# Attention values as f16 products for half of the units, and a new order of the step's four queues

## Chip, core, metric

The kernel runs on one core of a Trainium2 chip. The metric is the device time of one execution in microseconds (us), lower is better. The engines are PE (matmul, with its weight loads shown apart as PEld), DVE (vector), ACT (scalar activation), POOL (GpSimd) and SP, which issues most of the DMAs. Each engine runs its own instructions in the order written, and waits on semaphores for the others.

## What is computed

The input is x of 8 batches, 512 rows and 256 columns. After a layer norm, an attention with a compressive memory runs over four segments of 128 rows, with 16 heads of 64. An FFN of three coupled cycles follows. The change touches the attention alone:

```
scores  = mask(q @ k.T * scale)
att_dot = softmax(scores) @ v
att_mem = (elu(q) + 1) @ M / ((elu(q) + 1) @ Z)
M, Z    = M + (elu(k) + 1).T @ v,  Z + sum(elu(k) + 1)
out     = (gate * att_mem + (1 - gate) * att_dot) @ Wo
x       = x + layernorm(out)
```

## The kernel before

**Tiles.** Two batches make a pair, so there are 4 pairs of 4 segments, which gives 16 steps m = 4 * bp + s. A step handles 32 units (2 batches by 16 heads), in four groups g of 8 units. A group has two halves of 4 units, and its units are also split by par, 0 or 1, the two units that share one pair of 64 partitions. v has 65 columns a unit: 64 of v and a column of ones, so that the sum of the softmax comes out with the product.

**What a group does.** PE transposes q and k of the group (`turn`), ACT and DVE split them into f16 high and low parts, and `scores` makes the masked scores from 24 f16 products into the two PSUM banks `s_bank`, par 0 and par 1. DVE takes the row maxima, ACT the exponentials (`probs`), PE transposes them back into `s_bank` (`turn_probs`), and ACT copies them to `PT` (`take_p`). `read_out(g, half)` then multiplies PT with v for 4 units in f32 (L1305), the queries with the memory M (L1311), and after the second half the keys with v for the new memory (L1319). DVE divides (`divide`), POOL mixes with the gate (`gated`) and makes elu(k) + 1 (`elu_k`).

**What else is in a step.** The projections of the next step's q, k and v (`project` 0 to 5, 12 f16 products of 512 columns each, taken by DVE's `take_x`, L915), the transposes of the finished attention of the step before (`to_rows` on DVE, A0 to A3 on PE), the output projection Y (32 records at L1347), its layer norm and residual (y, x2), the next rows' layer norm (N) and the transposed result (F). They share two banks `t_bank` in turn, in the order of `STEP_JOBS`. The last step (m = 15) has no projections.

**What sets the order.** Every queue is written out by hand in the functions `step` of PE, DVE, ACT and POOL. There is one `s_bank`, so `scores` of a group waits until the probabilities of the group before have been copied. There is one `x_bank`, so each projection waits for the transpose of the one before. A step is counted below from its first score product (L1270 for g = 0). Step 9 lies at 509.43 to 562.61 us.

Of the kernel before, what the change touches and what calls it, by code (L numbers as in the profile page):

```python
# [45 lines left out]
STEP_JOBS = ["Q1", "K1", "A0", "A1", "A2", "A3", "Y", "Q2", "K2", "N", "Q3", "K3", "F", "Q0", "K0"]  # L46
# [18 lines left out]
def infini_block_kernel(nc, x, Wq, Wk, Wv, Wo, betas, memory0, z0, cw1, cb1, cw2, cb2, cw3, cb3,  # L65
                        cw4, cb4, gw1, gb1, gw2, gb2, gw3, gb3, adaptive_range, out):
    ctx = ExitStack()
    with ctx:
# [51 lines left out]
        PT = alloc(GU * P).rearrange("p (h j i) -> p h j i", h=2, j=GP)  # L120
# [4 lines left out]
        attT = alloc(2 * H * DK).rearrange("p (w j r) -> p w j r", w=2, j=8)  # L125
# [104 lines left out]
        p_done = sem("p_done")  # L230
# [77 lines left out]
        o_done, od_done = sem("o_done"), sem("od_done")  # L308

# [14 lines left out]
        with nc.Block() as block:  # L324
# [77 lines left out]
            def _(pool):  # L402
# [71 lines left out]

                def y_dev(bp, s):

                    deviation(r_rs, r_mv, y_stat, y_rstd, bp * NSEG + (s + 1))
# [10 lines left out]
                def step(bp, s):  # L488
                    m = bp * NSEG + s
                    elu_k(bp, s, 0)  # L490
                    if m > 0:
                        gated(*before(bp, s), 3, 0)
                        gated(*before(bp, s), 3, 1)
                    elu_k(bp, s, 1)
                    gated(bp, s, 0, 0)
                    gated(bp, s, 0, 1)
                    if m < NT - 2:
                        deviation(n_rs, n_mv, n_stat, n_rstd, m + 3)
                    y_dev(bp, s)
                    gated(bp, s, 1, 0)  # L500
                    residual(bp, s)
                    elu_k(bp, s, 2)
                    x2_dev(bp, s)
                    gated(bp, s, 1, 1)
                    elu_k(bp, s, 3)
                    gated(bp, s, 2, 0)
                    gated(bp, s, 2, 1)
# [73 lines left out]
            def _(act):  # L581
# [41 lines left out]
                def take_q(bp, s, g):  # L623
# [8 lines left out]
                    act.activation(eq, eq, ACT.Exp, scale=-1.0).then_inc(qk_act, 1)  # L632
                    b, n = t_job(bp, s, f"K{g}")
# [21 lines left out]
                def probs(bp, s, g):  # L655
                    G = 4 * s + g
                    for par in range(2):
                        act.wait_ge(m_done, bp * 32 + (2 * G + par + 1))
                        for j in range(GP):
                            last = act.activation(Pr[:, par, j, :], s_bank[:, par, j * P:(j + 1) * P], ACT.Exp,  # L660
                                                  bias=negm[:, par, j:j + 1])
                        last.then_inc(e_done, 1)

                def take_p(bp, s, g):
                    for par in range(2):
                        act.wait_ge(pt_full, bp * 32 + 8 * s + 2 * g + par + 1)
                        last = act.activation(PT[:, par, :, :].rearrange("p j i -> p (j i)"), s_bank[:, par, :],  # L667
                                              ACT.Copy)
                    last.then_inc(p_done, 1)
# [24 lines left out]
                def step(bp, s):  # L694
                    ahead, last = bp * NSEG + s < NT - 2, bp * NSEG + s == NT - 1
                    exp_k(bp, s, 0)
                    probs(bp, s, 0)
                    take_p(bp, s, 0)
                    if s == 0 and bp > 0:
                        reset(*before(bp, s), 3)  # L700
                    take_q(bp, s, 1)
# [3 lines left out]
                    probs(bp, s, 1)  # L705
                    take_a(t_job(bp, s, "A2"), 2)
                    take_a(t_job(bp, s, "A3"), 3)
                    take_p(bp, s, 1)
                    reset(bp, s, 0)
                    take_y(t_job(bp, s, "Y"))  # L710
                    take_q(bp, s, 2)
                    exp_k(bp, s, 2)
# [4 lines left out]
                    probs(bp, s, 2)  # L717
                    take_p(bp, s, 2)
                    take_q(bp, s, 3)
                    exp_k(bp, s, 3)  # L720
                    reset(bp, s, 1)
                    take_f(t_job(bp, s, "F"), bp * NSEG + (s - 1))
                    probs(bp, s, 3)
# [878 lines left out]
```

## Time and profile before

| what | value |
|---|---|
| median of three runs | 1071.33 us (1067.8 to 1072.13) |
| the profiled execution's own time | 1069.13 us |
| span from first to last instruction | 1067.3 us |
| first score product, m = 0 | at 34.97 us |
| first score product, m = 15 | at 826.97 us |
| mean granted TensorE clock | 0.98 of full speed |

The rest of the span is the start (weights and the first projections) and the FFN at the end. A busy time in the profile is the union of an engine's instructions. An f32 product appears as two records, so four products of `read_out` are "x8". Matmuls overlap in the records, so what a group costs is read from its start to the next group's start.

### The profile page before, as it was taken

To read this page: it belongs to the slowest core of one execution; us is meant where nothing else is said; L and a number is where in the kernel's file an instruction comes from. 1 tells how busy PE (TensorE), PEld (TensorE's weight loads), DVE (VectorE), ACT (ScalarE), POOL (GpSimd) and SP (SyncE) were. 2 spreads that over 40 slices of the span, in tenths; PEclk is the share of its full clock that TensorE was granted. 3 is DMA by queue.
4 is the path that set the end of the run, shared out by engine and by line. 5 is a ranking of instruction groups with operands and counts; after the bars stand their busy time and mean duration, and the time that the engine had idled before them with its cause. 6 is when DMAs were issued, how large, how long until landed. Compare 5 with 4: busy or idle time off the path is not lost.

```text
span 1067.3 us, 20188 instructions
## 1 busy us (share of the span) xinstructions
PE 989.8 (93%) x7748; PEld 697.6 (65%) x7748; DVE 780.9 (73%) x1400; ACT 634.6 (59%) x1364; POOL 577.8 (54%) x688
## 2 busy tenths in 40 slices
PE   5999999999999999999999999999999889999971
PEld 2677777776777777767777777777777765343431
DVE  6868686867787877777777777686868463588685
ACT  4756565556566564556565646574746354687872
POOL 4456565446565654456565634565656352455573
PEclk9999999999999999999999999999999899999995
DMA  7100000000000000000000000000000100300025
GB/s 187 32 21 1 21 2 20 3 22 1 21 2 21 2 20 2 21 2 21 1 21 2 21 2 20 2 21 1 12 2 10 24 11 10 157 1 1 1 44 115
DMA packets 17038, 23.92 MB, mean 22 GB/s; under 512 B 7472, under 2 KB 9264, under 8 KB 16432
## 3 DMA queue, kind: packets, MB, share of 16 engines
q1 hardware_dynamic: 15472, 18.58, 6.3%
q10 hardware_dynamic: 1472, 4.06, 1.1%
q8 instruction: 62, 1.02, 0.4%
q14 instruction: 32, 0.26, 0.1%
HBM read 13.97 MB, written 8.65 MB: 21 GB/s over the span
## 4 chain that ended last, share of the span: by engine, by line
PE 72%; DVE 18%; POOL 3%; ACT 3%; issue 3%; POOLq 0%; DVEq 0%; ACTq 0%
PE ps L1241 18%; PE ps L1347 11%; PE ps L1305 6%; PE ps L1282 5%; PE ps L1488 4%; PE ps L1475 4%; DVE arena L915 4%; PE ps L1311 3%; PE ps L1292 3%; PE ps L1332 3%; PE ps L1470 3%; PE ps L1257 3%; DVE arena L875 2%; PE ps L1319 2%; DVE arena L940 2%
## 5 line engine op out<-in xcount | busy, mean ns | idle before, releaser
L1241 PE MATMUL ps<-arena 128*128 128x512 f16 x1152 | 266.7, 382 | 5.1 <-DVE arena L892 3.0
L660 ACT ACTIVATE arena<-ps,arena 128x128 f32<-128x128 f32 x512 | 139.4, 387 | 96.1 <-DVE arena L940 96.1
L1241 PEld LDWEIGHTS ps<-arena 128*128 128x128 f16 x1152 | 110.3, 98 | 126.1 <-DVE arena L915 4.5
L915 DVE STREAM_TRANSPOSE arena<-ps 128x1024 f32<-128x1024 f32 x96 | 145.6, 1517 | 24.6 <-PE ps L1241 22.5
L468 POOL TENSOR_TENSOR arena<-arena 128x256 f32<-128x256 f32 x128 | 93.2, 729 | 123.2 <-DVE arena L950 82.0
L1305 PE MATMUL ps<-arena 128*128 128x65 f32 x1024 | 135.9, 276 | 5.9 <-ACT arena L667 4.8
L1305 PEld LDWEIGHTS ps<-arena 128*128 128x128 f32 x1024 | 127.4, 192 | 18.8 <-ACT arena L667 8.3
L867 DVE BATCH_NORM_STATS2 arena<-arena 128x6 f32<-128x256 f32 x100 | 36.9, 410 | 121.0 <-ACT arena L686 120.2
L1347 PE MATMUL ps<-arena 128*128 128x256 f32 x544 | 121.9, 382 | 0.0
L453 POOL TENSOR_TENSOR arena<-arena 128x512 f32<-128x512 f32 x48 | 73.2, 1525 | 86.6 <-ACT arena L653 86.6
L1347 PEld LDWEIGHTS ps<-arena 128*128 128x128 f32 x544 | 102.0, 190 | 15.7 <-ACT arena L674 0.8
L472 POOL TENSOR_TENSOR arena<-arena 128x256 f32<-128x256 f32 x128 | 95.3, 745 | 10.0
L421 POOL TENSOR_TENSOR arena<-arena 128x2 f32<-128x2 f32 x50 | 9.8, 196 | 167.3 <-DVE arena L871 167.3
L470 POOL TENSOR_TENSOR arena<-arena 128x256 f32<-128x256 f32 x128 | 93.6, 731 | 10.0
L667 ACT ACTIVATE arena<-ps 128x512 f32<-128x512 f32 x128 | 76.5, 614 | 33.6 <-PE ps L1292 33.6
L950 DVE TENSOR_TENSOR arena<-ps,arena 128x512 f32<-128x512 f32 x128 | 88.5, 691 | 4.4
L940 DVE TENSOR_REDUCE arena<-ps 128x4 f32<-128x512 f32 x128 | 80.8, 672 | 12.5 <-PE ps L1282 12.5
L1311 PE MATMUL ps<-arena 128*128 128x130 f32 x512 | 85.3, 289 | 0.0
L674 ACT ACTIVATE arena<-ps 128x512 f32<-128x512 f32 x68 | 37.0, 595 | 75.0 <-PE ps L1332 75.0
L1292 PE MATMUL ps<-arena 128*128 128x128 f32 x512 | 77.5, 279 | 4.3 <-ACT arena L660 4.3
L1257 PE MATMUL ps<-arena 128*128 128x128 f32 x512 | 77.2, 273 | 0.0
L875 DVE TENSOR_SCALAR arena<-arena 128x256 f32<-128x256 f32 x100 | 62.4, 664 | 18.4 <-POOL arena L423 18.0
(120 smaller groups left out, 1788.3 us busy)
## 6 DMA issues: line engine op xcount, KB each, us to landing
x_rows<-arena SPq DMA_DIRECT2D x17, 256.0 KB, 2.0
arena<-x_rows SPq DMA_DIRECT2D x4, 1024.0 KB, 7.8
arena<-in_L_attn_x_dram SPq DMA_DIRECT2D x124, 32.0 KB, 1.8
out_dram<-arena SPq DMA_DIRECT2D x18, 128.0 KB, 3.1
arena<-in_L_attn_Wq_dram ACTq DMA_DIRECT2D x2, 512.0 KB, 4.3
arena<-in_L_attn_Wk_dram ACTq DMA_DIRECT2D x2, 512.0 KB, 6.8
arena<-in_L_attn_Wv_dram ACTq DMA_DIRECT2D x2, 512.0 KB, 8.3
arena<-in_L_attn_Wo_dram SPq DMA_DIRECT2D x8, 128.0 KB, 4.6
```

What stands on the lines that cost most here:

```text
L468: pool.tensor_tensor(mem, mem, dot, ALU.subtract).then_inc(mix, 1)
L470: pool.tensor_tensor(mem, mem, gt, ALU.mult).then_inc(mix, 1)
L472: pool.tensor_tensor(att.rearrange("p (e y r h) -> p y h r e", y=2, r=2, h=HP)[:, g // 2, h:h + 2], mem, dot, ALU.add).then_inc(att_done, 1)
L660: last = act.activation(Pr[:, par, j, :], s_bank[:, par, j * P:(j + 1) * P], ACT.Exp, bias=negm[:, par, j:j + 1])
L915: dve.transpose(dst[:, d0:d0 + 32], bank.rearrange("p w (d c) -> p d w c", c=C)).then_inc(x_free, 1)
L940: dve.tensor_reduce(negm[:, par, :], s_bank[:, par, :].rearrange("p (j i) -> p j i", j=GP), AX.X, ALU.max, negate=True).then_inc(m_done, 1)
L1241: last = pe.matmul(bank[:, w, :], xc[:, lx, k, w * P:(w + 1) * P], W16[lw][:, k, i, :], start=(n == 0), stop=(n == 5))
L1257: last = pe.transpose(t_bank[b][:, j * P:(j + 1) * P], heads(src[par])[:, g // 2, GP * (g % 2) + j], identf)
L1292: last = pe.transpose(s_bank[:, par, j * P:(j + 1) * P], Pr[:, par, j, :], identf)
L1305: pe.matmul(pm_bank[:, 0, u * DV1:(u + 1) * DV1], PT[:, par, j, :], v[:, GP * (g % 2) + j, par, 0:DV1], start=True, stop=True)
L1311: last = pe.matmul(pm_bank[:, 1, a * 2 * DV1:(a + 1) * 2 * DV1], sqT[g % 2][:, j, :], M[:, GP * g + j, :, :], start=True, stop=True)
L1347: last = pe.matmul(t_bank[b][:, w * D:(w + 1) * D], attT[:, w, j, :], Wo_sb[:, j, :], start=(j == 0), stop=(j == 7))
```

## The change

For the units with par 0, probabilities and values are both split into an f16 high and an f16 low part, and their product is made of three f16 products (high high, high low, low high). Units with par 1 stay in f32. The high part of the probabilities is ACT's copy out of PSUM, which it made before in f32. The low part is a new DVE instruction, `low_p`, four a step. The parts of v are a new ACT instruction `v_high` and a new POOL instruction `v_low`, four a step each. `scores` waits for `low_p` too.

`read_out` becomes three functions: `recall` (memory product), `values` and `remember` (new memory). `maxima`, `probs`, `take_p` and `to_rows` are split in two halves each, `take_q` of ACT in `exp_q` and `high_k`. `project` can be issued in two halves of 6 products. attT now lies in the memory of nat. The queues of one step after the change, where d(g,h) is `divide`, q/k are `take_q`/`take_k`, x is `take_x`, p(g,par) stands for `probs` and t(g,par) for `take_p`, and a prime marks work of the step before:

```
PE    S0 recall/values/remember(3,1)' turnQ1 P0 turnK1 tp(0,0) recall(0,0) tp(0,1) P1 values(0,0) S1
      A0 A1 recall(0,1) A2 values(0,1) A3 remember0 turnQ2 tp(1,0) Y tp(1,1) turnK2 P2a N P2b
      recall/values(1,0) S2 P3 recall/values/remember(1,1) turnQ3 tp(2,0) turnK3 P4a tp(2,1) P4b
      recall/values(2,0) S3 F recall/values/remember(2,1) turnQ0 tp(3,0) P5a tp(3,1) recall(3,0)
      turnK0 P5b values(3,0)
DVE   max(0,0) max(0,1) d(3,1)' q1 x0 low_p0 rows0 k1 rows1 d(0,0) max(1,0) n_stats max(1,1) x1
      low_p1 d(0,1) q2 n_norm y_stats k2 y_norm x2 split d(1,0) max(2,0) x2_stats max(2,1) x3
      x2_norm d(1,1) low_p2 q3 k3 d(2,0) max(3,0) max(3,1) x4 d(2,1) seq_sums low_p3 q0 k0 d(3,0) x5
ACT   exp_k0 v_high0 exp_q1 p(0,0) p(0,1) t(0,0) v_high1 t(0,1) high_k1 exp_k1 A0 A1 p(1,0) A2 A3
      t(1,0) exp_k2 exp_q2 p(1,1) v_high2 y high_k2 exp_k3 n t(1,1) p(2,0) p(2,1) t(2,0) exp_q3
      t(2,1) high_k3 p(3,0) p(3,1) f t(3,0) exp_q0 v_high3 t(3,1) high_k0
POOL  v_low0 gated(3,0)' gated(3,1)' elu_k0 elu_k1 v_low1 gated(0,0) n_dev elu_k2 y_dev gated(0,1)
      residual x2_dev elu_k3 v_low2 gated(1,0) gated(1,1) gated(2,0) v_low3 gated(2,1)
```

The core of the diff (the four `step` functions are in the list above):

```diff
-STEP_JOBS = ["Q1", "K1", "A0", "A1", "A2", "A3", "Y", "Q2", "K2", "N", "Q3", "K3", "F", "Q0", "K0"]
+STEP_JOBS = ["Q1", "K1", "A0", "A1", "A2", "A3", "Q2", "Y", "K2", "N", "Q3", "K3", "F", "Q0", "K0"]
...
+        PT16 = alloc(GP * P, F16).rearrange("p (n j i) -> p n j i", n=2, j=GP)
+        PT32 = alloc(GP * P).rearrange("p (j i) -> p j i", j=GP)
         Pr = alloc(GU * P).rearrange("p (h j i) -> p h j i", h=2, j=GP)
...
-        attT = alloc(2 * H * DK).rearrange("p (w j r) -> p w j r", w=2, j=8)
+        attT = nat.rearrange("p w e c -> p (w e c)").rearrange("p (w j r) -> p w j r", w=2, j=8)
+        VE = DV1 + 1
+        vsplit = [alloc(UNITS // 2 * VE // 2, F16).rearrange("p (g h e) -> p g h e", g=GROUPS, h=GP)
+                  for _ in range(2)]
         identf = alloc(P)
...
+        def v_units(s, g):
+            return v_pos[s % 2].rearrange("p (y r h e) -> p y r h e", y=2, r=2, h=HP)[
+                :, g // 2, 0, GP * (g % 2):GP * (g % 2) + GP, 0:DV1]
...
+                def v_low(bp, s, g):
+                    pool.wait_ge(vh_done, 4 * (bp * NSEG + s) + g + 1)
+                    hi, lo = (v[:, g, :, 0:DV1] for v in vsplit)
+                    pool.tensor_tensor(lo, v_units(s, g), hi, ALU.subtract).then_inc(vl_done, 1)
...
+                def exp_q(bp, s, g):
                     b, n = t_job(bp, s, f"Q{g}")
...
+                def take_p(bp, s, g, par):
+                    dst = PT16[:, 0] if par == 0 else PT32
+                    act.wait_ge(pt_full, bp * 32 + 8 * s + 2 * g + par + 1)
+                    act.activation(dst.rearrange("p j i -> p (j i)"), s_bank[:, par, :],
+                                   ACT.Copy).then_inc(p_copied, 1)
+                def v_high(bp, s, g):
+                    m = bp * NSEG + s
+                    act.wait_ge(x_free, 6 * m + 6)
+                    if m > 0:
+                        act.wait_ge(pm_full, 8 * (m - 1) + 2 * g + 2)
+                    act.activation(vsplit[0][:, g, :, 0:DV1], v_units(s, g), ACT.Copy).then_inc(vh_done, 1)
...
+                    G = bp * 16 + 4 * s + g
+                    hi, lo = (PT16[:, n].rearrange("p j i -> p (j i)") for n in range(2))
+                    dve.wait_ge(p_copied, 2 * G + 1)
+                    dve.tensor_tensor(lo, s_bank[:, 0, :], hi, ALU.subtract).then_inc(p_low, 1)
                 def divide(bp, s, g, half):
...
                     xc = xcur[par]
-                    for w in range(2):
+                    for w in ws:
...
+                    if 1 in ws:
+                        last.then_inc(x_full, 1)
                 def turn(bp, s, g, which="QK"):
...
                         pe.wait_ge(t_free[b], n + 1)
-                    pe.wait_ge(p_done, bp * 16 + G + 1)
+                    if bp * 16 + G > 0:
...
-                def read_out(bp, s, g, half):
-                    n = 8 * s + 2 * g + half
-                    v = v_pos[s % 2].rearrange("p (y r h e) -> p y h r e", y=2, r=2, h=HP)[:, g // 2]
-                    pe.wait_ge(p_done, bp * 16 + 4 * s + g + 2)
-                    if g == 0:
-                        pe.wait_ge(x_free, bp * 24 + 6 * s + 6)
-                    pe.wait_ge(pm_free, bp * 32 + n + 1)
-                    for u in range(4):
-                        j, par = 2 * half + u // 2, u % 2
-                        pe.matmul(pm_bank[:, 0, u * DV1:(u + 1) * DV1], PT[:, par, j, :],
-                                  v[:, GP * (g % 2) + j, par, 0:DV1], start=True, stop=True)
...
                         pe.wait_ge(m_reset, bp * 8 + 2 * (g + 1))
                     for a in range(2):
                         j = 2 * half + a
-                        last = pe.matmul(pm_bank[:, 1, a * 2 * DV1:(a + 1) * 2 * DV1], sqT[g % 2][:, j, :],
-                                         M[:, GP * g + j, :, :], start=True, stop=True)
-                    if half == 1 and s < NSEG - 1:
-                        pe.wait_ge(sk_done, sk_count(bp, s, g) + 2)
-                        for a in range(GP):
-                            h = GP * (g % 2) + a
-                            for par in range(2):
-                                unit = 2 * (GP * (g - g % 2) + h) + par
-                                last = pe.matmul(pm_bank[64 * par:64 * par + 64, a // 2,
-                                                         (4 + a % 2) * DV1:(5 + a % 2) * DV1],
-                                                 sk[:, DK * unit:DK * (unit + 1)], v[:, h, par, 0:DV1],
-                                                 start=True, stop=True)
+                        pe.matmul(pm_bank[:, 1, a * 2 * DV1:(a + 1) * 2 * DV1], sqT[g % 2][:, j, :],
+                                  M[:, GP * g + j, :, :], start=True, stop=True)
+                def values(bp, s, g, half):
+                    G = bp * 16 + 4 * s + g
+                    v = v_pos[s % 2].rearrange("p (y r h e) -> p y h r e", y=2, r=2, h=HP)[:, g // 2]
+                    pe.wait_ge(p_copied, 2 * (G + 1))
+                    pe.wait_ge(p_low, G + 1)
+                    pe.wait_ge(vl_done, G + 1)
+                    for a in range(2):
+                        j = 2 * half + a
+                        for i, (lp, lv) in enumerate(((0, 0), (0, 1), (1, 0))):
+                            pe.matmul(pm_bank[:, 0, 2 * a * DV1:(2 * a + 1) * DV1], PT16[:, lp, j, :],
+                                      vsplit[lv][:, g, j, 0:DV1], start=(i == 0), stop=(i == 2))
+                        last = pe.matmul(pm_bank[:, 0, (2 * a + 1) * DV1:(2 * a + 2) * DV1], PT32[:, j, :],
+                                         v[:, GP * (g % 2) + j, 1, 0:DV1], start=True, stop=True)
+                    if half == 0 or s == NSEG - 1:
+                        last.then_inc(pm_full, 1)
+                def remember(bp, s, g):
```

## Rows read from the trace of the kernel before

**Rows 1.** The page's first part: busy time of each engine.
```profile
PE 989.8 (93%) x7748; PEld 697.6 (65%) x7748; DVE 780.9 (73%) x1400; ACT 634.6 (59%) x1364; POOL 577.8 (54%) x688
```
**Rows 2.** Busy times by stretch: steps 8, 9 and 11, then step 15.
```profile
core 0: us, PE busy (x) PEld busy (x) DVE busy (x) ACT busy (x) POOL busy (x), PEclk, DMA share, GB/s
455.76:509.43 53.67, 51.15 (x449) 38.87 (x449) 40.44 (x75) 33.36 (x74) 32.95 (x40) 1.00 0.03 11
509.43:562.61 53.18, 51.88 (x467) 39.41 (x466) 41.06 (x76) 32.01 (x71) 32.51 (x40) 1.00 0.04 11
...
615.74:667.15 51.41, 50.12 (x417) 37.80 (x416) 38.28 (x71) 28.78 (x71) 21.45 (x31) 1.00 0.03 11
827.00:878.00 51.00, 41.67 (x356) 34.60 (x355) 27.99 (x54) 25.06 (x62) 21.98 (x32) 0.93 0.07 18
```
**Rows 3.** Timeline of PE in step 9: start us, duration us, group.
```profile
509.77 0.84 PE L1282 MATMUL ps<-arena 64*128 64x128 f16 x24
510.54 1.11 PE L1305 MATMUL ps<-arena 128*128 128x65 f32 x8
511.48 0.67 PE L1311 MATMUL ps<-arena 128*128 128x130 f32 x4
512.08 0.69 PE L1319 MATMUL ps<-arena 128*64 128x65 f32 x16
512.70 2.76 PE L1241 MATMUL ps<-arena 128*128 128x512 f16 x12
515.30 0.60 PE L1292 MATMUL ps<-arena 128*128 128x128 f32 x4
...
519.63 1.00 PE L1305 MATMUL ps<-arena 128*128 128x65 f32 x8
520.47 0.67 PE L1311 MATMUL ps<-arena 128*128 128x130 f32 x4
...
552.11 0.63 PE L1216 MATMUL ps<-arena 128*128 128x128 f32 x4 [0.80 <-DVE arena L925]
```
**Rows 4.** Weight loads of step 9 by line and form.
```profile
L1305 PEld LDWEIGHTS ps<-arena 128*128 128x128 f32 x64 | 7.9, 191 | 1.0 <-ACT arena L667 0.4
L1241 PEld LDWEIGHTS ps<-arena 128*128 128x128 f16 x72 | 6.8, 98 | 7.6 <-DVE arena L915 0.3
```
**Rows 5.** DVE instructions of step 9 by line and form.
```profile
L1006 DVE STREAM_TRANSPOSE arena<-arena 128x1024 f32<-128x1024 f32 x2 | 2.4, 1224 | 0.3 <-POOL arena L472 0.3
...
L892 DVE TENSOR_TENSOR arena<-ps,arena 128x512 f16<-128x512 f32 x1 | 0.7, 681 | 0.0
```
**Rows 6.** Timeline of DVE, in the middle and near the end of step 9.
```profile
520.51 0.67 DVE L933 SCALAR_TENSOR_TENSOR arena<-ps,arena 128x512 f16<-128x512 f32 x1
521.17 0.21 DVE L947 RECIPROCAL arena<-ps 128x8 f32<-128x8 f32 x1
521.41 0.69 DVE L950 TENSOR_TENSOR arena<-ps,arena 128x512 f32<-128x512 f32 x1
522.02 1.24 DVE L915 STREAM_TRANSPOSE arena<-ps 128x1024 f32<-128x1024 f32 x1
523.19 1.25 DVE L940 TENSOR_REDUCE arena<-ps 128x4 f32<-128x512 f32 x2
...
556.90 0.85 DVE L958 TENSOR_TENSOR arena<-ps,arena 64x260 f32<-64x260 f32 x2
557.79 2.07 DVE L915 STREAM_TRANSPOSE arena<-ps 128x1024 f32<-128x1024 f32 x1
559.89 0.69 DVE L924 SCALAR_TENSOR_TENSOR arena<-ps,arena 128x512 f32<-128x512 f32 x1
```
**Rows 7.** Timeline of ACT in step 9.
```profile
517.30 0.59 ACT L628 ACTIVATE arena<-ps 128x512 f16<-128x512 f32 x1
...
518.95 0.58 ACT L635 ACTIVATE arena<-ps 128x512 f16<-128x512 f32 x1
...
524.07 2.18 ACT L660 ACTIVATE arena<-ps,arena 128x128 f32<-128x128 f32 x8
```
**Rows 8.** ACT instructions of the run by line and form.
```profile
L619 ACT ACTIVATE arena<-arena 64x260 f32<-64x260 f32 x32 | 13.3, 416 | 0.5
```
**Rows 9.** POOL instructions of the run by line and form.
```profile
L472 POOL TENSOR_TENSOR arena<-arena 128x256 f32<-128x256 f32 x128 | 95.3, 745 | 10.0
```
**Rows 10.** Timeline of PE, early in step 12.
```profile
679.51 0.40 PE L1270 MATMUL ps<-arena 64*64 64x512 bf16 x2 [1.38 <-DVE arena L925]
```

More of the change, by code:

```diff
@@ L489, in step @@
                     m = bp * NSEG + s
-                    elu_k(bp, s, 0)
+                    v_low(bp, s, 0)
                     if m > 0:
@@ L696, in step @@
                     exp_k(bp, s, 0)
-                    probs(bp, s, 0)
-                    take_p(bp, s, 0)
+                    v_high(bp, s, 0)
+                    exp_q(bp, s, 1)
+                    probs(bp, s, 0, 0)
+                    probs(bp, s, 0, 1)
+                    take_p(bp, s, 0, 0)
+                    v_high(bp, s, 1)
+                    take_p(bp, s, 0, 1)
                     if s == 0 and bp > 0:
                         reset(*before(bp, s), 3)
-                    take_q(bp, s, 1)
+                    high_k(bp, s, 1)
                     exp_k(bp, s, 1)
@@ L704, in step @@
                     take_a(t_job(bp, s, "A1"), 1)
-                    probs(bp, s, 1)
+                    probs(bp, s, 1, 0)
                     take_a(t_job(bp, s, "A2"), 2)
                     take_a(t_job(bp, s, "A3"), 3)
-                    take_p(bp, s, 1)
-                    reset(bp, s, 0)
+                    take_p(bp, s, 1, 0)
+                    exp_k(bp, s, 2)
+                    exp_q(bp, s, 2)
+                    probs(bp, s, 1, 1)
+                    v_high(bp, s, 2)
                     take_y(t_job(bp, s, "Y"))
-                    take_q(bp, s, 2)
-                    exp_k(bp, s, 2)
+                    high_k(bp, s, 2)
+                    exp_k(bp, s, 3)
                     if ahead:
@@ L716, in step @@
                         replicate()
[L717 to L720, printed above, removed]
+                    take_p(bp, s, 1, 1)
+                    reset(bp, s, 0)
+                    probs(bp, s, 2, 0)
+                    probs(bp, s, 2, 1)
+                    take_p(bp, s, 2, 0)
+                    exp_q(bp, s, 3)
+                    take_p(bp, s, 2, 1)
                     reset(bp, s, 1)
+                    high_k(bp, s, 3)
+                    probs(bp, s, 3, 0)
+                    probs(bp, s, 3, 1)
                     take_f(t_job(bp, s, "F"), bp * NSEG + (s - 1))
-                    probs(bp, s, 3)
-                    take_p(bp, s, 3)
+                    take_p(bp, s, 3, 0)
                     if not last:
-                        take_q(bp, s, 0)
+                        exp_q(bp, s, 0)
+                    v_high(bp, s, 3)
+                    take_p(bp, s, 3, 1)
                     reset(bp, s, 2)
-                act.sem_inc(p_done, 1)
-                take_q(0, -1, 0)
+                    if not last:
+                        high_k(bp, s, 0)
+                act.wait_ge(init, 5)
+                exp_q(0, -1, 0)
+                high_k(0, -1, 0)
                 act.wait_ge(m_in, 64)
@@ L1000, in seq_sums, with to_rows @@
                         dve.tensor_tensor(to, gacc, gpart, ALU.add).then_inc(gs_done, 1)
-                def to_rows(n):
+                def to_rows(n, halves=(0, 1)):
                     dve.wait_ge(att_done, n)
-                    for e in range(2):
+                    for e in halves:
                         dve.transpose(nat.rearrange("p w e c -> p e w c")[:, 32 * e:32 * e + 32, :, :],
@@ L1047, in step @@
                     divide(bp, s, 2, 0)
-                    maxima(bp, s, 3)
-                    seq_sums(bp, s)
-                    divide(bp, s, 2, 1)
+                    maxima(bp, s, 3, 0)
+                    maxima(bp, s, 3, 1)
                     if not last:
                         take_x(bp, s, 4)
+                    divide(bp, s, 2, 1)
+                    seq_sums(bp, s)
+                    low_p(bp, s, 3)
+                    if not last:
                         take_q(bp, s, 0)
```

169 lines of the change are left out of this document (103 added, 66 removed).

## The prediction

> **What bounds the kernel now.** I read the page first, for how busy each engine is. PE is busy 93% of the span, DVE 73% [rows 1]. Then I split the attention part by the first score product of each step and asked for busy times by stretch. A middle step takes 53.18 us and PE is busy 51.88 of it at the full clock, DVE 41.06, ACT 32.01, POOL 32.51. The step after a segment-3 step takes 53.67, a segment-3 step, which has no new memory, 51.41 [rows 2]. So PE sets the pace, and DVE is the second engine, at 77%.
>
> The timeline of PE says how much of that is work. A group costs the distance to the next group's start. Giving each group of step 9 its shortest distance, I get 51.4 us (of which projections 6 x 2.60, Y 7.0, value products 7.1, memory products 4.7, four scores 4.4). Then 1.8 us of the step are stalls. Some show as gaps (0.80 us in front of L1216 [rows 3]), the rest is hidden under the modelled ends. The projection of 12 f16 products of 512 columns runs from 512.70 to 515.30, 217 ns a product, which is the columns at full rate: nothing of a weight load shows there [rows 3].
>
> **The change, part by part.**
>
> *Value products.* Eight calls a step had 4 f32 products each. A call takes 0.94 us (510.54 to 511.48) or 0.84 us (519.63 to 520.47) [rows 3], so one f32 product costs 210 to 235 ns, say 225. Half of the 32 go: 16 x 0.225 = 3.6 us off a step. In come 48 f16 products of 65 columns with 128x128 f16 weights, which the trace does not show. Bounds: the columns at the projection's rate, 65/512 x 217 = 28 ns, plus some 11 ns of start that I read from it, give 39 ns. The scores run 24 products of 128 columns in 0.77 us [rows 3], which is 32 ns each, but two of them sit side by side in the array, so a pair, each with a load of its own and twice our columns, takes 64 ns. A weight load of 128x128 f16 is recorded with 98 ns, one of f32 with 191 ns [rows 4]. If nothing covered it, 98 ns would be the price; but an f32 record of 65 columns comes every 118 ns (0.94/8) though its load is recorded with 191, so a record's length is not its price. The kinds of load differ by 93 ns a record, and 118 - 93 is below even the bound of the columns. So I take 50 ns, between 39 and 64: 48 x 0.050 = 2.4 us. The net is -1.2 us a step (-1.7 at 39, -0.5 at 64, +1.1 at 98). Over 15 steps this is -18 us (-26 to -8, and +16). The Trainium skill (TensorE: Matmul & The Clock Gate, Back-to-back issue gap) gives 81 ns for a stream of load and product pairs at 128 columns. By it the term would be +0.3 us a step. The scores' 32 ns a product are below that, but they are row-tiled.
>
> *DVE.* `low_p` reads PSUM and writes 128x512 f16, as L892 does in 681 ns [rows 5], 0.6 to 0.68 us of queue: 4 a step, +2.5 us, 43.5 in all. *ACT.* `v_high` is 260 elements wide. L619 with 260 takes 416 ns [rows 8], so +1.7 us, 33.7 in all. *POOL.* `v_low` is like L472, 745 ns [rows 9], so +3.0 us, 35.5 in all. *PE halves of projections* add no product. *attT in nat* costs nothing, as `take_a` writes what PE has just read. No DMA moves. These three costs are hidden if PE stays the bound. What they can do is come late in a chain.
>
> *Order.* I walked the new queues through a step, with t = 0 at the first score product. DVE prices are distances [rows 6]: `maxima` 0.6 a half, `take_k` 0.66, `take_q` 1.2, first-half `divide` 0.85 (521.17 to 522.02), second-half 1.7 (with 0.89 at L958), `take_x` 1.17 for q and k and 2.1 for v (557.79 to 559.89), `to_rows` 1.2 a half [rows 5]. ACT: `exp_q` 1.65 (517.30 to 518.95), `probs` 1.09 a half [rows 7], copies 0.6. PE as in rows 3, transposes 0.44, values 0.75. PE work is 50.2 us. These places are close:
>
> - Start of the step: `take_x` 5 ends at 3.1, only then can DVE do the maxima. `exp_q1` runs 3.6 to 5.3, `probs` 5.3 to 7.5, PE wants them at 6.5 and 7.6: met. `take_x` 0 stands behind maxima, `divide`(3,1) and `take_q` 1 and ends at 8.4, P1 wants it at 8.0: 0.45 us of stall.
> - S1 at 11.7 needs `low_p0` (9.0) and `take_k` 1 (10.8). `take_k` 1 no longer waits for both transposes: met. A0 at 12.8 needs the second one, 11.9: met.
> - Y hides `low_p1` (18.5), `take_q` 2 and `n_norm`. After Y, `take_p`(1,1) stands behind y, `high_k2`, `exp_k3` and n on ACT and ends at 28.8 where values(1,0) wants it at 28.7: 0.1.
> - S2 at 29.5, `take_x` 2 at 29.5, `take_x` 3 at 34.7 (P4 at 36.4), `low_p2` 38.0, S3 at 40.8 against `take_k` 3 at 40.4: met.
> - End: `take_x` 4 ends at 45.35, P5a wants it at 45.2. turnK0 wants the bank that `seq_sums` frees at 48.0, 0.25 late. S0 of the next step wants `take_k` 0 at 50.4: met.
>
> POOL runs ahead of each of its deadlines by over 2 us, save `gated`(3,1)', done at 8.9 just as the first `to_rows` could start. New stalls come to 0.95 us, with some issue gaps 1.15. Against 1.8 this is -0.65 a step, x 15 = -10 us (0 to -27: at best all stalls go).
>
> *Step after segment 3.* There S1 waited 1.38 us for `take_q`, which stood behind `to_rows` [rows 10]; in the new order both transposes are no longer ahead of it. That frees about 1.2 us in three steps, of which `reset` ahead of `high_k0` and `high_k1` takes some back: -2 us.
>
> *Last step.* PE is busy 41.67 of 51.00 there [rows 2], so a faster PE buys nothing. Four `low_p` in the chain scores, maxima, probs, copy, scores cost up to 2.4 us, the earlier `take_q` gives back as much: 0 (-2 to +3). Start and FFN are unchanged.
>
> Sum against the profiled execution's own 1069.1 us (span 1067.3 and 1.8 around it): -18 - 10 - 2 + 0 = -30, so 1039. The median of the runs shown is 2.2 us higher, 1071.3, so the forecast is 1041 us, 51.3 us a middle step.
>
> **Rivals.**
>
> 1. *DVE becomes the bound.* From the end of S3 to the end of the next `take_x` 0, DVE's queue has no idle place: 16.6 us of work by the prices above, where PE has 16.3. DVE at 43.5 of 51.3 speaks for it. The 12 us that DVE idles today speak against it, though most of that is around Y, not here. If its prices there are 7% more than I take (L915 writes v in 2.07 and q in 1.24 [rows 6], so they do vary), each step loses 1.2 us: 1041 + 18 = 1059.
> 2. *The f16 product costs the middle of 64 and 98, 81 ns*, load and product in turn. Then the term is +0.3 a step instead of -1.2: 1041 + 22 = 1063. It is also what the section of the Trainium skill (TensorE: Matmul & The Clock Gate, Back-to-back issue gap) would make of the time.
> 3. *Slower: weight loads lie open.* Each f16 product has weights of its own, and only 65 columns to cover the next load, where a projection has 512. At the recorded 98 ns the term is +1.1 a step, +16, with order and resets 1071.3 + 16 - 12 = 1075, and with the columns after the load (98 + 28 = 126 ns) it is +2.4 us a step, +37 - 12: 1096, which I take for this rival. It decides above some 90 ns a product, where 48 products cost the 3.6 us of the f32 ones and the 0.65 that the order gives. For it: the record's 98. Against it: the f32 record's 118 with a load of 191.
> 4. *All of it works*: 39 ns, and hardly a stall. 50 us a middle step, 1022.
>
> **Numbers.** Forecast (1030 to 1052) 0.50, rival 1 0.14, rival 2 0.11, rival 3 0.12, rival 4 0.13. A measurement of this kernel can tell about 0.5%, 5.4 us, from no change. Of the 0.25 of rivals 1 and 2, 0.07 lies within it, their upper tails. So faster is 0.50 + 0.13 + 0.18 = 0.81, same 0.07, slower 0.12. The range is 1024 to 1066: it reaches to rivals 1, 2 and the upper half of rival 4, and leaves out rival 3 and the rest of rival 4. The forecast's own range is 1030 to 1052.
>
> **What would show it.** Distance between first score products: 51.3 us in a middle step (rival 1: 52.5, rival 4: 50). A values call of 2 f32 and 6 f16 products takes 0.75 us to the next group (0.68 at 39 ns, 0.83 at 64, 0.94 at 81, 1.04 and more in rival 3). By stretch DVE is busy 43.5, ACT 33.7, POOL 35.5 us. PE's waits in a middle step name L915 in front of P1 and P5, and `seq_sums` in front of turnK0. S1 after a segment-3 step no longer waits 1.38 us. I am wrong if PE's idle time per step is over 2.5 us, or if a values call takes longer than the 0.89 of before.

## The result and the profile after

The changed kernel takes 1026.97 us (median, 1026.6 to 1027.22) where the kernel before took 1069.78 us in the runs beside it: a ratio of 0.960, 95% interval 0.958 to 0.962. The gain is 42.8 us where 30 were forecast. The time lies inside the range on record (1024 to 1066), outside the narrower one of the likeliest case (1030 to 1052), and close to rival 4.

The page's first part, to be held against [rows 1]:

```profile
PE 958.7 (94%) x8004; PEld 677.2 (66%) x8004; DVE 825.9 (81%) x1464; ACT 654.1 (64%) x1428; POOL 614.8 (60%) x752
```

Busy times by stretch, cut at the first score product of steps 8, 9 and 11 and of the last step, as in [rows 2]:

```profile
core 0: us, PE busy (x) PEld busy (x) DVE busy (x) ACT busy (x) POOL busy (x), PEclk, DMA share, GB/s
438.00:487.94 49.94, 49.41 (x464) 37.70 (x465) 43.00 (x78) 34.59 (x79) 34.45 (x43) 1.00 0.04 12
487.94:538.66 50.72, 50.21 (x481) 38.28 (x480) 43.93 (x79) 33.18 (x76) 34.78 (x43) 1.00 0.04 12
...
589.44:639.10 49.66, 47.96 (x435) 36.40 (x434) 41.18 (x75) 29.71 (x74) 24.15 (x36) 1.00 0.04 12
789.93:839.00 49.07, 40.76 (x377) 33.60 (x377) 32.56 (x66) 27.04 (x69) 25.74 (x38) 0.93 0.08 19
```

Step 9 went from 53.18 to 50.72 us, the step after segment 3 (step 8) from 53.67 to 49.94, the step of segment 3 from 51.41 to 49.66. The 15 steps with projections, from the first score product of step 0 to that of step 15, took 792.0 us (34.97 to 826.97) and take 754.5 (35.48 to 789.93). That is 37.5 of the 42.1 us by which the spans of the two profiles differ (1067.3 and 1025.2). The stretch behind the first score product of step 15 gave 5.1 us, 2.9 of them ahead of the scores of group 3 (before 41.2 us after the step's start, now 38.3), and the start took 0.5 more.

DVE is busy 43.93 us of step 9 (43.5 forecast), ACT 33.18 (33.7), POOL 34.78 (35.5). Timeline of PE at `values`(0,0), step 9:

```profile
498.72 0.26 PE L1379 MATMUL ps<-arena 128*128 128x65 f16 x3
498.81 0.41 PE L1381 MATMUL ps<-arena 128*128 128x65 f32 x2
499.06 0.26 PE L1379 MATMUL ps<-arena 128*128 128x65 f16 x3
499.15 0.41 PE L1381 MATMUL ps<-arena 128*128 128x65 f32 x2
499.49 0.41 PE L1334 MATMUL ps<-arena 64*64 64x512 bf16 x2
```

Three f16 products take 0.09 us (498.72 to 498.81), 30 ns each, and the f32 product that follows takes 0.25. The call takes 0.77 us, where it took 0.84 to 0.94 [rows 3]. The one gap that the view of waits shows in step 9 is in front of the scores of group 3. They start 0.1 us after DVE has ended `take_k` 3 (the second line):

```profile
529.22 0.40 PE L1334 MATMUL ps<-arena 64*64 64x512 bf16 x2 [0.51 <-issue]
528.44 0.68 DVE L979 SCALAR_TENSOR_TENSOR arena<-ps,arena 128x512 f16<-128x512 f32 x1
```

### The profile page after: what moved, and what is told of

It reads as the page before. It is cut to its first block, busy times and chain, and to the rows that moved or that the text cites. A ratio compares the mean times of both kernels' runs of the same rounds, so it can differ in the third digit from the quotient of the medians.

```text
span 1025.2 us, 21046 instructions
## 1 busy us (share of the span) xinstructions
PE 958.7 (94%) x8004; PEld 677.2 (66%) x8004; DVE 825.9 (81%) x1464; ACT 654.1 (64%) x1428; POOL 614.8 (60%) x752
## 4 chain that ended last, share of the span: by engine, by line
PE 88%; DVE 5%; ACT 3%; issue 2%; POOL 1%; POOLq 0%; DVEq 0%
PE ps L1302 24%; PE ps L1424 11%; PE ps L1319 7%; PE ps L1381 6%; PE ps L1356 6%; PE ps L1366 5%; PE ps L1346 5%; PE ps L1569 4%; PE ps L1582 4%; PE ps L1396 3%; PE ps L1409 3%; PE ps L1564 3%; PE ps L1379 2%; PE ps L1334 2%; PE ps L1277 1%
## 5 line engine op out<-in xcount | busy, mean ns | idle before, releaser
L1302 PE MATMUL ps<-arena 128*128 128x512 f16 x1152 | 274.4, 383 | 5.5 <-DVE arena L938 3.1
L682 ACT ACTIVATE arena<-ps,arena 128x128 f32<-128x128 f32 x512 | 141.9, 375 | 116.6 <-DVE arena L985 116.6
L1424 PEld LDWEIGHTS ps<-arena 128*128 128x128 f32 x544 | 102.2, 190 | 13.8 <-ACT arena L702 0.8
L489 POOL TENSOR_TENSOR arena<-arena 128x260 f16<-128x260 f32 x64 | 42.7, 666 | 113.1 <-ACT arena L697 113.1
L478 POOL TENSOR_TENSOR arena<-arena 128x256 f32<-128x256 f32 x128 | 93.2, 728 | 19.4 <-DVE arena L1001 19.4
L689 ACT ACTIVATE arena<-ps 128x512 f16<-128x512 f32 (+1 forms) x128 | 77.0, 602 | 36.2 <-PE ps L1356 36.0
L480 POOL TENSOR_TENSOR arena<-arena 128x256 f32<-128x256 f32 x128 | 93.3, 729 | 10.0
L1381 PE MATMUL ps<-arena 128*128 128x65 f32 x512 | 96.8, 289 | 0.0
L985 DVE TENSOR_REDUCE arena<-ps 128x4 f32<-128x512 f32 x128 | 83.1, 672 | 10.1 <-PE ps L1346 10.1
L463 POOL TENSOR_TENSOR arena<-arena 128x512 f32<-128x512 f32 x48 | 73.4, 1529 | 22.8 <-ACT arena L676 22.8
L921 DVE TENSOR_SCALAR arena<-arena 128x256 f32<-128x256 f32 x100 | 76.7, 808 | 12.1 <-POOL arena L433 12.1
L1319 PE MATMUL ps<-arena 128*128 128x128 f32 x512 | 84.5, 288 | 0.7 <-ACT arena L702 0.7
L1356 PE MATMUL ps<-arena 128*128 128x128 f32 x512 | 79.1, 277 | 4.0 <-ACT arena L682 4.0
L1366 PE MATMUL ps<-arena 128*128 128x130 f32 x512 | 80.0, 278 | 1.0 <-DVE arena L1001 1.0
L1366 PEld LDWEIGHTS ps<-arena 128*128 128x128 f32 x512 | 71.2, 192 | 10.1 <-DVE arena L1001 1.4
L1381 PEld LDWEIGHTS ps<-arena 128*128 128x128 f32 x512 | 77.6, 192 | 0.0
```

The lines of the kernel that those rows point to most:

```text
L478: pool.tensor_tensor(mem, mem, dot, ALU.subtract).then_inc(mix, 1)
L480: pool.tensor_tensor(mem, mem, gt, ALU.mult).then_inc(mix, 1)
L1302: last = pe.matmul(bank[:, w, :], xc[:, lx, k, w * P:(w + 1) * P], W16[lw][:, k, i, :], start=(n == 0), stop=(n == 5))
L1319: last = pe.transpose(t_bank[b][:, j * P:(j + 1) * P], heads(src[par])[:, g // 2, GP * (g % 2) + j], identf)
L1356: last = pe.transpose(s_bank[:, par, j * P:(j + 1) * P], Pr[:, par, j, :], identf)
L1366: pe.matmul(pm_bank[:, 1, a * 2 * DV1:(a + 1) * 2 * DV1], sqT[g % 2][:, j, :], M[:, GP * g + j, :, :], start=True, stop=True)
```

## The experiments

All were timed in rounds against the kernel before (median 1069.8 to 1071.5 us in the rounds), so the ratios can be compared. Step 9 is read from each profile, from its first score product to the next step's.

| kernel | median us | ratio to before (95%) | step 9, us | DVE busy |
|---|---|---|---|---|
| before | 1069.8 | 1 | 53.18 | 41.06 |
| changed | 1027.0 | 0.960 (0.958 to 0.962) | 50.72 | 43.93 |
| order_alone | 1035.8 | 0.967 (0.964 to 0.969) | 51.36 | 41.72 |
| values_alone | 1106.3 | 1.033 (1.030 to 1.035) | 54.78 | 42.98 |
| products_twice | 1039.9 | 0.972 (0.969 to 0.974) | 51.46 | 44.11 |
| high_only | 1011.5 | 0.946 (0.943 to 0.948) | 49.82 | 41.77 |
| low_p_beside | 1043.1 | 0.974 (0.972 to 0.976) | 51.83 | 46.06 |
| rows_together | 1056.1 | 0.986 (0.984 to 0.989) | 52.26 | 43.98 |
| projections_whole | 1065.2 | 0.995 (0.993 to 0.997) | 53.21 | 43.66 |
| order_alone_whole | 1082.9 | 1.010 (1.006 to 1.014) | 54.19 | 41.60 |
| recall_behind | 1053.2 | 0.984 (0.983 to 0.986) | 52.30 | 43.81 |
| norm_later | 1026.1 | 0.958 (0.956 to 0.960) | 50.44 | 42.82 |
| all_f16 | 1070.0 | 0.999 (0.998 to 1.001) | 53.02 | 46.26 |
| all_f16_eased | 1049.8 | 0.981 (0.978 to 0.984) | 51.55 | 45.82 |

**The two halves of the change.** The first theory, read from the trace after, was that each half has a share of its own, and the f16 products the larger one. `order_alone` undoes the products in the changed kernel, and takes out `low_p`, `v_high` and `v_low`:

```diff
-                        for i, (lp, lv) in enumerate(((0, 0), (0, 1), (1, 0))):
-                            pe.matmul(pm_bank[:, 0, 2 * a * DV1:(2 * a + 1) * DV1], PT16[:, lp, j, :],
-                                      vsplit[lv][:, g, j, 0:DV1], start=(i == 0), stop=(i == 2))
+                        pe.matmul(pm_bank[:, 0, 2 * a * DV1:(2 * a + 1) * DV1], PT0[:, j, :],
+                                  v[:, GP * (g % 2) + j, 0, 0:DV1], start=True, stop=True)
```

> The new order of the four queues with all value products in f32, and without the low and high parts of the values and probabilities. Theory A (the two parts each have their own share: f16 products take 1.7 us of PE work off a step, the order takes 0.7 to 1.0 us of stalls off): 26 us of the 43 are lost again, 1052 to 1057 us. Rival B (the order is what counts, and the f16 products only shift work from PE to DVE): within 10 us of the changed kernel, 1027 to 1037 us.

`values_alone` is the kernel before with the products, and the splitting instructions in its old queues (`low_p` behind `take_x` 0, `n_stats`, `x2_norm` and `divide`(2,1), `v_high` ahead of `probs`, `v_low` behind `elu_k`):

```diff
                     if not last:
                         take_x(bp, s, 0)
+                    low_p(bp, s, 0)
                     to_rows(bp * 32 + 8 * s + 8)
```

> The order of the kernel before, with the value products of par 0 as three f16 products, and the splitting instructions put into the old queues. Theory A, the parts add up: 26 us under the kernel before, 1043 to 1047 us. Rival C (the old order can't take up 2.5 us more of DVE a step: scores wait for low_p behind other DVE work): the gain is half of that or less, 1055 to 1072 us, and PE's waits name DVE.

Measured: 1035.8 and 1106.3. Theory A fell on both sides. The order alone gives 35 us of the 43. The products alone, in this placing, cost 36. Only behind the new order do they give their 9 us. Step 9 of both in busy times by stretch, first order_alone:

```profile
491.86:543.22 51.36, 51.36 (x465) 39.89 (x464) 41.72 (x75) 32.09 (x72) 32.54 (x39) 1.00 0.04 12
```

then values_alone, and the waits of PE in that step:

```profile
530.61:585.39 54.78, 50.72 (x481) 37.55 (x480) 42.98 (x79) 33.26 (x75) 34.81 (x44) 1.00 0.04 11
```

```profile
PE ps L1350 <- issue: 2.0, 1, 2.0
PE ps L1313 <- DVE arena L956: 0.9, 1, 0.9
PE ps L1282 <- DVE arena L946: 0.6, 1, 0.6
PE ps L1350 <- ACT arena L688: 0.4, 1, 0.4
```

In order_alone PE is never seen idle, and its step of 51.36 us is close to the 51.4 of work that I had added up for the kernel before. Not all of the 1.82 us between the steps are stalls: the eight calls of value and memory products take 11.4 us here, by distances, and took 11.8 in that sum (7.1 and 4.7). So by distances some 0.4 us are lighter work and some 1.4 are stalls. Why these calls are lighter no run shows (recall_behind, below, finds no such gain with f16 products), and what small delays still hide under the modelled ends the trace does not tell.

In values_alone PE stands 4.1 us of the step, in front of value products (L1350), scores (L1313) and projections (L1282). The largest gap, 2.0 us, is in front of the value products of group 2, at 573.30. They start 0.1 us after DVE has ended `low_p`, which stood behind `x2_norm`:

```profile
573.30 0.25 PE L1350 MATMUL ps<-arena 128*128 128x65 f16 x3 [1.98 <-issue]
572.51 0.69 DVE L978 TENSOR_TENSOR arena<-ps,arena 128x512 f16<-128x512 f32 x1
```

So rival C was right in kind and too mild. Another placing of `low_p` in the old queues may do better; it was not tried.

**The price of an f16 product.** `products_twice` issues each set of three twice:

```diff
-                        for i, (lp, lv) in enumerate(((0, 0), (0, 1), (1, 0))):
+                        for i, (lp, lv) in enumerate(((0, 0), (0, 1), (1, 0)) * 2):
...
-                                      vsplit[lv][:, g, j, 0:DV1], start=(i == 0), stop=(i == 2))
+                                      vsplit[lv][:, g, j, 0:DV1], start=(i % 3 == 0), stop=(i % 3 == 2))
```

> The changed kernel with each set of three f16 products issued twice (the second set overwrites the first), 48 more f16 products of 65 columns a step. Theory A (30 ns each, read from three products in 0.09 us in the trace): 48 x 0.030 x 16 = +23 us, less what falls into stalls, 1045 to 1051 us. Rival, the price of the prediction (50 ns): +38 us, 1065 us. Rival, 39 ns: +30 us, 1057 us.

Its timeline at `values`(0,0):

```profile
503.96 0.34 PE L1379 MATMUL ps<-arena 128*128 128x65 f16 x6
504.14 0.41 PE L1381 MATMUL ps<-arena 128*128 128x65 f32 x2
504.39 0.34 PE L1379 MATMUL ps<-arena 128*128 128x65 f16 x6
504.57 0.41 PE L1381 MATMUL ps<-arena 128*128 128x65 f32 x2
504.91 0.40 PE L1334 MATMUL ps<-arena 64*64 64x512 bf16 x2
```

Six products take 0.18 us: 30 ns again. The same place in order_alone, where both units are in f32:

```profile
502.77 0.33 PE L1346 MATMUL ps<-arena 128*128 128x65 f32 x2
502.94 0.39 PE L1348 MATMUL ps<-arena 128*128 128x65 f32 x2
503.16 0.39 PE L1346 MATMUL ps<-arena 128*128 128x65 f32 x2
503.38 0.39 PE L1348 MATMUL ps<-arena 128*128 128x65 f32 x2
503.70 0.40 PE L1302 MATMUL ps<-arena 64*64 64x512 bf16 x2
```

The call takes 0.93 us there and 0.77 in the changed kernel, 0.16 less, 1.3 us a step: close to the 1.2 of the prediction, with other parts. An f16 product costs 30 ns and not 50, but the f32 product behind one costs 250 ns where it costs 220 behind another f32. The whole kernel grew by 13 us and not by the 23 expected, since 0.7 of the 1.44 us a step fell into stalls: step 9 is 0.74 us longer, and its gap in front of the scores of group 3 is gone.

**Who owns the stall that is left.** `high_only` drops `low_p`, `v_low` and two of the three products, so the low parts are missing from par 0:

```diff
-                        for i, (lp, lv) in enumerate(((0, 0), (0, 1), (1, 0))):
+                        for i, (lp, lv) in enumerate(((0, 0),)):
...
```

> The changed kernel with the low parts left out: par 0 has one f16 product (high by high) instead of three, and low_p and v_low are gone, v_high stays. Theory H (the 0.6 us of stall a step that the changed kernel has over its PE work come from the low parts on DVE): with 32 f16 products of 30 ns less and no stall, 50.72 - 0.96 - 0.6 = 49.2 us a step, 1002 to 1006 us. Rival (the stalls are of the order, not of the low parts): 49.8 us a step, 1010 to 1014 us.

49.82 us a step and 1011.5 us, the rival's numbers: the step falls by 0.9 us, what the products give and no more. That does not show that the low parts on DVE, 2.2 us of its time, cost a middle step nothing. The run takes work off both engines. `take_k` 3 starts 39.70 us into the step where it started at 40.50, so without the low parts it comes 0.8 us earlier, but PE gets to the scores of group 3 earlier too, by 0.6 us. The gap in front of them shrinks from 0.51 to 0.27 us, and P1 and P5a come 0.17 and 0.13 us later behind the transposes ahead of them than they did. What the low parts cost at an unchanged PE, no run shows. `low_p_beside` adds the same DVE work once more:

```diff
                     dve.wait_ge(p_copied, 2 * G + 1)
+                    dve.tensor_tensor(junk[g], s_bank[:, 0, :], hi, ALU.subtract)
```

> The changed kernel with each low part of the probabilities computed once more, into a buffer that nothing reads, ahead of the true one: 4 more DVE instructions of 0.6 us a step. Theory E (in the changed kernel DVE has become the second bound: it stood idle 6.8 us of a step there and 6.8 us in the kernel with all values in f16 too, so its busy time plus 6.8 us sets the step): 2.4 us a step, 1060 to 1066 us. Rival (PE sets the pace and only one or two waits a step get longer): 1030 to 1045 us.

DVE was busy 2.1 us more and the step grew by 1.1, the whole by 16 us, as the rival had it. So theory E fell as a sum: that DVE stood idle 6.8 us in two kernels was a coincidence (5.8 here). The extra work costs where a wait ends last, and that is two places: the scores of group 3 (0.95 us in place of 0.51) and the first scores of a step, where the changed kernel had no gap. From PE's timeline (L1336 is the first score product), the start of step 9, its scores of group 3 and the start of step 10:

```profile
495.55 0.40 PE L1336 MATMUL ps<-arena 64*64 64x512 bf16 x2 [0.55 <-issue]
537.39 0.40 PE L1336 MATMUL ps<-arena 64*64 64x512 bf16 x2 [0.95 <-DVE arena L972]
547.38 0.40 PE L1336 MATMUL ps<-arena 64*64 64x512 bf16 x2 [0.47 <-issue]
```

**Which moves of the order count.** `rows_together` puts the start of DVE's queue back:

```diff
-                    take_q(bp, s, 1)
                     if not last:
                         take_x(bp, s, 0)
                     low_p(bp, s, 0)
-                    to_rows(bp * 32 + 8 * s + 8, (0,))
+                    to_rows(bp * 32 + 8 * s + 8)
+                    take_q(bp, s, 1)
                     take_k(bp, s, 1)
-                    to_rows(bp * 32 + 8 * s + 8, (1,))
```

> The changed kernel with the start of DVE's queue in the old sub-order: take_q 1 behind take_x 0 and both transposes to_rows, take_k 1 last. Theory: take_k 1 ends 1.2 us later in each step, which the margin in front of the scores of group 1 (0.9 us in my walk) does not cover, and in the steps after segment 3 the old wait of 1.4 us comes back: 0.2 to 0.5 us in a middle step, over 1 us in three, 1031 to 1039 us. Rival (the margins elsewhere take it up): 1026 to 1029 us.

It cost 29 us, more than expected. Its waits of PE in step 9 (L1333 is the first score product, L971 is in `take_q`):

```profile
PE ps L1333 <- DVE arena L971: 1.5, 1, 1.5
PE ps L1333 <- issue: 0.5, 1, 0.5
```

The scores of group 1 wait 1.5 us in a middle step (the 0.5 are those of group 3, as before), which is the wait that [rows 10] shows only after segment 3. `projections_whole` issues projections 2, 4 and 5 in one piece (4 is shown), and `order_alone_whole` does the same to order_alone:

```diff
-                        project(bp, s, 4, (0,))
+                        project(bp, s, 4)
                     turn_probs(bp, s, 2, 1)
-                    if not last:
-                        project(bp, s, 4, (1,))
...
```

> The changed kernel with projections 2, 4 and 5 issued in one piece instead of in halves (2 in front of N, 4 in front of the second turn of group 2's probabilities, 5 behind the transpose of k 0). Theory E: PE work is the same, but the second half of the turned probabilities and the transposes come up to 1.3 us later for DVE and ACT, which have no room there: 0.5 to 1 us a step, 1035 to 1043 us. Rival (halves make no difference): 1025 to 1030 us.

> The new order with all value products in f32 (as in order_alone) and projections 2, 4 and 5 in one piece. Theory F (the halves matter in themselves: they bring the turned probabilities and the transpose of k forward, with or without low parts): order_alone's step of 51.36 us grows by 1.5 to 2.5 us, 1059 to 1072 us. Rival G (they only make room for the low parts on DVE): less than 0.6 us a step, 1035 to 1044 us.

They cost 38 us, and 47 us without the low parts. Both rivals fell, and E and F were too mild: 2.5 us a step where E had up to 1, and 2.8 where F had up to 2.5. Waits of PE in step 9 of projections_whole:

```profile
PE ps L1366 <- DVE arena L1009: 1.1, 1, 1.1
PE ps L1379 <- ACT arena L689: 1.0, 2, 0.7
PE ps L1334 <- issue: 0.4, 1, 0.4
```

`values` (L1379, groups 1 and 2) waits for ACT's copies of the turned probabilities. In group 1 the copy stands behind ACT's n, for which PE now transposes after all of projection 2, in group 2 it waits for a turn behind all of projection 4. `recall` (L1366) waits for `divide`. With f32 values and whole projections the old order (1069.9) is faster than the new one (1082.9): the halves are part of this order, and whether they would gain anything in the old one was not tried.

`recall_behind` issues the memory product behind the values, as `read_out` did:

```diff
-                    recall(bp, s, 0, 0)
                     turn_probs(bp, s, 0, 1)
...
                     values(bp, s, 0, 0)
+                    recall(bp, s, 0, 0)
```

> The changed kernel with recall issued right behind values, as read_out had it, not ahead. PE work: the memory product ahead takes 0.45 us to the next group in the trace of the changed kernel, behind the values it took 0.59. Theory: 0.1 us a call, 8 calls, and PE has less to do while values wait: 0.8 to 1.5 us a step, 1040 to 1051 us. Rival (the distance is only shared out otherwise between the two): 1026 to 1032 us.

It cost 26 us. Its timeline at `values`(0,0):

```profile
509.74 0.26 PE L1381 MATMUL ps<-arena 128*128 128x65 f16 x3
...
510.42 0.67 PE L1365 MATMUL ps<-arena 128*128 128x130 f32 x4
511.01 0.40 PE L1334 MATMUL ps<-arena 64*64 64x512 bf16 x2
```

Values and memory product take 1.27 us together. The changed kernel takes 0.77 for the values and 0.45 to 0.55 for the memory product, and over the eight calls of step 9 the two kernels differ by no more than 0.1 us (10.1 each, the gap in front of the scores of group 3 left out). So the price of a call is only shared out otherwise, as the rival had it, and the theory's 0.1 us a call fell. Nearly all of the 1.58 us of the step are waits:

```profile
PE ps L1356 <- ACT arena L682: 0.4, 1, 0.4
PE ps L1319 <- DVE arena L1039: 0.3, 1, 0.3
PE ps L1409 <- ACT arena L702: 0.3, 1, 0.3
PE ps L1381 <- ACT arena L689: 0.3, 1, 0.3
```

Each of the four is in front of a group that had the memory product ahead of it before: the second turn of group 0's probabilities (L1356), A2 (L1409), values(1,0) (L1381) and turn K0 (L1319). By distances they cost 0.5 to 0.6 us each, 2.1 in all. A memory product ahead of a wait fills it.

**Versions beyond.** `norm_later` moves `x2_norm` on DVE behind `take_k` 3:

```diff
-                    x2_norm(bp, s)
                     divide(bp, s, 1, 1)
                     low_p(bp, s, 2)
                     take_q(bp, s, 3)
                     take_k(bp, s, 3)
+                    x2_norm(bp, s)
```

> The changed kernel with the second layer norm's DVE instructions (x2_norm) moved behind take_k 3, ahead of divide(2,0). Theory E: the gap of 0.5 us in front of the scores of group 3 goes, since take_k 3 comes 1.2 us earlier, and the transpose F behind these scores still finds its rows ready: 0.3 to 0.5 us a step, 1019 to 1023 us. Rival: the DVE work is only pushed on into the stretch up to the next projection 1, which has no room: 1025 to 1032 us.

The gap in front of the scores of group 3 is gone and the step takes 50.44 us, but the median is 1026.1, not theory E's 1019 to 1023: with these intervals that can't be told from the changed kernel. In the two profiles the 15 steps take 3.0 us less (751.4 against 754.5), and the stretch behind the scores of group 3 of the last step takes 3.0 us more (200.0 against 196.9, more on this stretch below). `all_f16` has par 1 in f16 as well, `all_f16_eased` adds to it norm_later's move and an earlier second low part of group 0 (shown):

```diff
                     low_p(bp, s, 0)
+                    low_p(bp, s, 0, 1)
                     to_rows(bp * 32 + 8 * s + 8, (0,))
                     take_k(bp, s, 1)
-                    low_p(bp, s, 0, 1)
```

> The changed kernel with the units of par 1 also as three f16 products: 16 more f32 products a step become 48 f16 ones, DVE gets four more low parts (2.5 us a step, 46.5 of 50), ACT and POOL split twice the values. Theory A (PE sets the pace, and four waits of about 0.7 us for the second low part take some back): 1.7 us of PE off a step, 1.0 to 1.4 back, 1015 to 1024 us. Rival D (DVE is close enough to the bound that more of it costs its full 2.5 us): 1035 to 1050 us.

> All values in f16 (as in all_f16), with x2_norm moved behind take_k 3 and the second low part of group 0 ahead of to_rows. Theory (the waits of 1.1 us and 1.6 us in front of the value products of groups 0 and 2 are waits for DVE's place in the queue, not for its total): 2 us a step less than all_f16's 53.0, 1030 to 1042 us. Rival (DVE, busy 46.3 us a step, can't go under 52.5): 1060 to 1070 us.

Step 9 of each in busy times by stretch, all_f16 first:

```profile
510.13:563.15 53.02, 48.49 (x496) 35.76 (x497) 46.26 (x84) 34.40 (x76) 37.48 (x44) 1.00 0.04 11
```

```profile
494.74:546.29 51.55, 48.73 (x497) 35.90 (x497) 45.82 (x84) 33.77 (x75) 36.69 (x43) 1.00 0.05 12
```

PE's busy time fell to 48.5 us, and PE then stood 4.5 us. At 1070.0 us both theory A (1015 to 1024) and rival D (1035 to 1050) of all_f16 were too mild. Easing two places took 1.5 us of the step back where 2 were expected (1049.8 us, expected 1030 to 1042), and the step is under 52.5, so it was no floor of DVE's total; but neither version reaches the changed kernel. The waits that are left in front of values are those of groups 1, 2 and 3 (0.77, 0.38 and 0.55 us), and each ends 0.1 us after DVE's second low part, as here in group 1:

```profile
523.81 0.52 PE L1384 MATMUL ps<-arena 128*128 128x65 f16 x12 [0.77 <-issue]
523.03 0.68 DVE L991 TENSOR_TENSOR arena<-ps,arena 128x512 f16<-128x512 f32 x1
```

ACT's copy for it had ended at 522.87, so it is again a place in DVE's queue that is late.

## Why the prediction was right, and what in it was off

*What bounds the kernel* held: PE. In a middle step it is busy 50.21 of 50.72 us.

*Value products*: -1.2 us a step was forecast, and PE's work fell by 1.3. Two errors cancelled, so the size is in part luck. The price of an f16 product, 50 ns, was 30, which is 1.0 us a step less. Against it stand what I left out, that an f32 product behind an f16 one costs 30 ns more (some 0.4 us a step), and that the f32 products that went cost 195 ns (0.17 and 0.22 us in order_alone) and not 225 (0.5 us). My lower bound of 39 ns was no bound: the 11 ns that I added as a fixed start no row shows, and with 65 columns it does not occur. Of these 1.3 us a step the kernel keeps only 0.64 (51.36 to 50.72 from order_alone), about 9 us in all: most of the rest became the stall in front of the scores of group 3. The Trainium skill (TensorE: Matmul & The Clock Gate, Wait — 56ns, not 53.3ns?) gives columns / 2.4 GHz + 2.5 ns from start to start, which by my estimate is 29.6 ns for 65 columns; the trace agrees, with 30. Its 81 ns for pairs of load and product at 128 columns (Back-to-back issue gap) no run here shows.

*Order*: the step that failed is "New stalls come to 0.95 us, with some issue gaps 1.15. Against 1.8 this is -0.65 a step". order_alone showed no gap at all and -1.82 us a step, 27 us over 15 steps where I had put 10. Some 1.4 of the 1.82 are stalls, and some 0.4 are lighter calls of value and memory products, which I had not priced. My walk named P1, values(1,0), P5a and turn K0 as late. Of these the trace after shows P5a at most: 0.60 us lie between the start of turn_probs(3,0) and P5a (533.21 to 533.81) where 0.44 are its work. Instead the scores of group 3 were late, which I had as met (40.4 against 40.8). `take_k` 3 ended at 41.2, and ahead of it `x2_norm`, for which my list has no price, took 2.41 us where it took 1.74 in the kernel before (below). `norm_later` takes it out of the way and the gap goes. Elsewhere the walk was too pessimistic. That it was so by small latencies which I gave each hand-over is my reading, and no run tests it.

*After segment 3*: -2 us in three steps was forecast. Step 8 fell by 3.73 us where step 9 fell by 2.46, so 1.3 a step and 3.8 in all. The steps of segment 3 fell by less, 1.75 us (step 11), which the forecast did not tell apart. *Last step*: 0 was forecast, 2.9 us came up to the scores of group 3. Behind these scores another 2.2 us came that I can't place: over the profiles of all runs this stretch lies between 196.7 us (high_only) and 201.2 (recall_behind), it is 200.0 in norm_later, whose code behind that point is the changed kernel's but for the place of `x2_norm`, and 199.1 in the kernel before, so it may be no effect of the change.

The sum then reads -37.5 (15 steps) - 2.9 - 2.2 + 0.5 = -42.1 us, where -30 was forecast.

*Rivals.* 1, DVE as the bound: the busy time came as forecast, and DVE is no bound as a total: it idles 6.8 us of the step, and 2.1 us more of it in low_p_beside cost 1.1. But single places in its queue do set the pace, `take_k` 3 in the changed kernel and the low parts in all_f16. 2 and 3, a price of 81 or 126 ns: fell. 4, all of it works: nearest, in the time (1022 forecast, 1027 measured) and in the price of a product; its 50 us a step were 50.7. I gave it 0.13, and held the new order's stalls against it without a row that showed them.

## What to carry over

When one engine is busy 97% of a step and the rest is small waits, the order of the queues can be worth more than the work: here 35 us against 9, and the lighter products in the old order, in the one placing tried, made the kernel 3% slower. A change that moves work from the bound engine to others has to be priced with the waits that it makes at the single shared buffers, not by busy shares. Three f16 products of 65 columns take 0.09 us here and one f32 product 0.17 to 0.25, so even at 65 columns the three are cheaper on PE.

## What the hardware showed unasked

A product of 65 columns with a 128x128 f16 weight load of its own starts every 30 ns, though the load is recorded with 107 ns in step 9: most of the load is hidden even there. (Of each three products two load the same high part; all three loads are in the trace.) It holds in a longer row as well: the twelve f16 products of a call in all_f16, 0.52 us from the first start to the last end with 0.19 us for one, start within 0.33 us. An f32 product of 65 columns, two records, takes 0.22 us behind another f32 product and 0.25 behind f16 ones.

`x2_norm`, two DVE instructions of 128x256, took twice as long in one place as in another, in DVE's timeline of the changed kernel, and in norm_later:

```profile
522.58 2.41 DVE L921 TENSOR_SCALAR arena<-arena 128x256 f32<-128x256 f32 x2
```

```profile
525.09 1.19 DVE L921 TENSOR_SCALAR arena<-arena 128x256 f32<-128x256 f32 x2
```

In the first POOL works at `elu_k` (L463 at 521.96 for 1.54 us and L465 behind it), in the second at `gated` (L478, L480). In step 9 of the kernel before it took 1.74 (548.91), with `gated` on POOL. The changed kernel has the same pair of instructions for another layer norm, `n_norm`, at a place where POOL has just ended its work (at 510.76) and stands idle:

```profile
510.68 0.73 DVE L921 TENSOR_SCALAR arena<-arena 128x256 f32<-128x256 f32 x2
```

So the pair takes 0.73 us with POOL idle, 1.19 to 1.74 beside `gated`, whose instructions take 0.73 us each, and 2.41 beside `elu_k`, whose instructions take 1.54 and 1.27. It goes with what POOL runs beside it. Whether it is the length of POOL's instructions or the operands that they read, or where these lie, was not tried.
